# A chain of eight transformer layers on one core: a new order of the attention stages' work over two projection banks, masks and reciprocals moved between engines

## The reference, cut to what matters

```python
x = x + attn(ln(x), ln(x), 16 heads of 16, causal)      # SELF0
x = x + attn(ln(x), ctx,   16 heads of 16)              # CROSS0
x = x + mlp(ln(x))                                      # MLP0, 256 -> 1024 -> 256
x = x + attn(ln(x), ctx,   weights quantized)           # CROSS1
x = x + attn(ln(x), ln(x), logits + mask_SxS_fc0)       # SELF2
x = x + attn(ln(x), ctx,   16 heads of 16)              # CROSS2
x = x + mlp(ln(x))                                      # MLP2
x = x + attn3(ln(x), ln(ctx), 16 heads of 64, causal)   # SELF3
```

## Time and profile before

| | us |
|---|---|
| median of 3 runs (4729.28 to 4740.4) | 4730.53 |
| the profiled execution's own time | 4764.75 |
| its span in the trace | 4762.5 |
| granted TensorE clock, mean share | 0.928 |

### The profile page before, as it was taken

One profiled execution on the slowest core, in us unless ns is written; L12 is line 12 of the kernel. 1 busy time (PEld: TensorE's weight loads), 2 busy tenths in 40 slices (PEclk: granted clock), 3 DMA queues, 4 the chain that ended last, 5 costly groups with the idle time before them and its releaser, 6 DMA issues. The chain is left out here.

```text
span 4762.5 us, 66873 instructions
## 1 busy us (share of the span) xinstructions
PE 4395.3 (92%) x22610; PEld 2204.7 (46%) x22610; DVE 2705.0 (57%) x6114; ACT 2286.0 (48%) x4789; POOL 1240.6 (26%) x1277
## 2 busy tenths in 40 slices
PE   5999999999896899999999999999799899999998
PEld 3555543333463333334444443333266455555555
DVE  3555567776113677777777677777311344444443
ACT  2444456666220565654444445666421455455553
POOL 1111111111221111111111111111121566566664
PEclk8888889998797899999999999999699999999999
DMA  4433433443001443433232224443100000000000
GB/s 103 69 55 62 66 73 70 75 70 53 16 0 26 90 71 73 67 57 72 40 51 40 51 40 87 68 79 63 45 0 22 6 5 10 10 10 10 10 6 10
DMA packets 115318, 217.95 MB, mean 46 GB/s; under 512 B 22320, under 2 KB 25008, under 8 KB 113328
## 3 DMA queue, kind: packets, MB, share of 16 engines
q1 hardware_dynamic: 114992, 213.79, 24.7%
HBM read 39.11 MB, written 4.19 MB: 9 GB/s over the span
## 5 line engine op out<-in xcount | busy, mean ns | idle before, releaser
L901 ACT ACTIVATE Pr<-ST 128x512 f32<-128x512 f32 (+3 forms) x2560 | 1358.8, 564 | 1329.9 <-PE ST L486 1047.8
L486 PE MATMUL ST<-stk 50*128 50x512 f32 (+3 forms) x2560 | 1118.1, 486 | 17.1 <-ACT Pr L901 11.2
L1083 DVE TENSOR_REDUCE mx<-MX 128x1 f32<-128x512 f32 (+3 forms) x1408 | 855.9, 630 | 477.5 <-PE MX L486 469.9
L486 PE MATMUL MX<-stk 48*128 48x512 f32 (+3 forms) x1760 | 773.6, 475 | 114.3 <-DMA stk<-lo 75.2
L486 PE MATMUL OV<-Pr,V 128*32 128x512 f32 (+3 forms) x5120 | 710.5, 630 | 1.5 <-ACT Pr L901 1.5
L486 PEld LDWEIGHTS MX<-stk 48*128 48x128 f32 x1760 | 331.4, 201 | 724.7 <-issue 351.6
L1402 POOL TENSOR_SCALAR Pr<-Pr,mx 128x128 f32<-128x128 f32 (+3 forms) x512 | 548.3, 1083 | 386.7 <-DVE mx L1221 386.7
L486 PEld LDWEIGHTS ST<-stk 50*128 50x128 f32 x2560 | 462.9, 200 | 145.4 <-ACT Pr L901 112.9
L1083 DVE TENSOR_REDUCE mx<-OV 128x1 f32<-128x512 f32 (+3 forms) x640 | 400.4, 626 | 148.4 <-PE OV L486 148.2
L1336 POOL CAST mhl<-mx 128x16 fp32r<-128x16 f32 x160 | 31.9, 199 | 1475.7 <-DVE mx L1083 1124.4
L1333 POOL TENSOR_TENSOR X<-X,brow 128x1024 f32<-128x1024 f32 (+1 forms) x56 | 132.3, 2362 | 1015.9 <-DVE X L1035 1015.9
(11 more groups left out here) (134 smaller groups left out, 6781.6 us busy)
## 6 DMA issues: line engine op xcount, KB each, us to landing
stk<-hi SPq DMA_DIRECT2D x640, 128.0 KB, 3.9
stk<-lo SPq DMA_DIRECT2D x320, 128.0 KB, 4.0
misc<-misc SPq DMA_DIRECT2D x160, 128.0 KB, 3.8
sums<-misc SPq DMA_DIRECT2D x160, 128.0 KB, 4.1
misc<-in_ctx_t SPq DMA_DIRECT2D x24, 512.0 KB, 5.1
W_even<-in_w SPq DMA_DIRECT2D x4, 1024.0 KB, 6.0
W_even<-in_w SPq DMA_DIRECT2D x2, 2048.0 KB, 8.9
XH<-in_ctx_rows SPq DMA_DIRECT2D x8, 512.0 KB, 4.1
```

The costliest lines, as they stand in the source:

```text
L486: return nc.tensor.matmul(o, l, r, start=start, stop=stop)
L901: nc.scalar.activation(Pr[:, i % 2, h, q0:S], ST[h % 2][:, q0:S], ACT.Exp).then_inc(ex_done, 1)
L1083: nc.vector.tensor_reduce(m, bank[:, 0:k_n], AX.X, ALU.max).then_inc(mx_red, 1)
```

## The change

Five parts, quoted below: (a) the jobs go over two banks, LA for T0, K and V0, LB for T1, Q and V1, four jobs each, beside the turned maxima and the output projection in LB, with new places for all; LayerNorm's statistics and its GpSimd work go into the odd slot ahead of the turn; (b) DMAs in SyncE's queue are reordered, the maxima's rows last; (c) the sums are moved compactly (`few`, 128 x 32 per unit), inverted by one instruction, written to DRAM, and read back spread over 16 partitions per head; (d) in SELF0 no mask matmuls: VectorE adds `later0` in the reduction, and GpSimd clears the triangle of `Pr` after the exponential, ahead of the value product, which now is issued at j = 3 in SELF0; (e) in SELF2 VectorE masks heads 0 and 2. SELF3's mask tile is made from `later0` in one instruction; start-up loses four DMAs and two casts.

```diff
-        MASKED_BY_PE = (1, 2, 3)
+        MASKED_BY_PE = (1, 3)
...
-        J_T, J_K, J_Q, J_V, JOBS = 0, (2, 6), (3, 7), 4, 8
+        J_T, J_KQ, J_V, JOBS = 0, (1, 2), 3, 4
...
@@ SyncE, slot
                     if on["stack1"]:
-                        stack(U + 1, 1 - half, 1, GB + half)
+                        for kind in range(2):
+                            stack(U + 1, 1 - half, 1, GB + half, kind)
                     if on["tail"]:
                         move(U - 1, 1 - half, 1, GB - 1 + half)
+                        spread_rows(U - 1, 1 - half)
                     if on["b"]:
                         max_rows(U, half, 1)
-                    if on["m"]:
-                        max_rows(U + 1, 1 - half, 0)
-                    if on["a"]:
-                        stack(U + 2, half, 0, GB + 1)
-                    if on["b"]:
-                        move(U, half, 0, GB)
+                    if on["tail"]:
+                        widen(U - 1, 1 - half)
+                    if cross and half == 0 and 0 <= b < NB - 2:
+                        sp.wait_ge(lb_full, JOBS * (GB + 1))
+                        load_ctx(b + 2, c // 2)
+                    if on["a"]:
+                        for kind in range(2):
+                            stack(U + 2, half, 0, GB + 1, kind)
+                    if on["b"]:
+                        move(U, half, 0, GB)
+                    if on["m"]:
+                        max_rows(U + 1, 1 - half, 0)
...
-                    sp.dma_start(sums[64 * g:64 * g + 64, half, :], ovs[1:P:2, g, :]).then_inc(ov_moved[g], 16)
+                    sp.dma_start(few[64 * g:64 * g + 64, half, :], ovs[1:P:32, g, :].rearrange("h (c n) -> h c n", n=32)).then_inc(ov_moved[g], 16)
+
+                def spread_rows(U, half):
+
+                    sp.wait_ge(recip_done, U + 1)
+                    sp.dma_start(spread[half].rearrange("h (c n) -> (h c) n", n=32), few[:, half, :]).then_inc(spread_out, 16)
+
+                def widen(U, half):
+                    waits(sp, (spread_out, 16 * (U + 1)), (at_ready, BASE + U))
+                    rows = spread[half].rearrange("h (a n) -> h a n", a=1).broadcast_to([2 * G, HD, S])
+                    sp.dma_start(sums[:, half, :], rows).then_inc(spread_in, 16)
...
@@ TensorE, slot
-                            if at == (4, 2) and on["m"]:
+                            if at == (5, 2) and on["m"]:
+                                freed(2 + half)
                                 turn_max(U + 1, 1 - half, 0, 2 * (GB - 1 + half))
...
+                                if half == 0 and at == (0, 2):
+                                    wait(pe, la_free, JOBS * GB1 + J_T)
+                                    transpose_x(sa, ba, 0, LA).then_inc(la_full, 1)
...
+                                k_at = 1 if half == 0 else 0
+                                if at in ((k_at, 2), (k_at + 1, 2)):
...
+                                    project(LA, la_full, wq(sa, 1), half, source, i - k_at)
+                                if at in (((3, 2), (3, 3)) if half == 0 else ((2, 2), (3, 2))):
...
+                                    project(LB, lb_full, wq(sa, 0), half, hT, c)
+                                if half == 1 and i >= 4 and j == 2:
...
+                                    project_values(bank, full, wq(sa, 2), source, (i - 4) // 2, i % 2)
...
-                    pe.wait_ge(ex_done, 4 * (8 * U + i + 1))
+                    pe.wait_ge(*((cleared, 8 * U + i + 1) if causal else (ex_done, 4 * (8 * U + i + 1))))
...
@@ VectorE, slot
+                            if at == (1, 3) and on["tail"]:
+                                invert(U, 1 - half)
+                            if at in (((3, 1), (4, 2)) if half == 0 else ((2, 2), (4, 1))) and on["a"]:
+                                low_part(sa, U, half, int(i == 4))
...
+                            if at in ((6, 0), (7, 3)) and half == 1 and on["a"]:
+                                values_out(sa, GB + 1, 1 - par, i - 6)
...
+                    elif causal:
+                        k_n = P * (qt + 1)
+                        nc.vector.tensor_tensor_reduce(bank[:, 0:k_n], bank[:, 0:k_n], later0[:, S - k_n:S], 1.0, -3.0e38,
+                                                       ALU.add, ALU.max, m).then_inc(mx_red, 1)
...
+                def invert(U, half):
+
+                    for g in range(2):
+                        dve.wait_ge(ov_moved[g], 32 * U)
+                    nc.vector.reciprocal(few[:, half, :], few[:, half, :]).then_inc(recip_done, 1)
...
@@ GpSimd, slot
+                    if on["tail"] and ATTN[s - 1 if u == 0 else s][1]:
+                        clear(U - 1, 7)
...
+                def clear(U, i):
+
+                    waits(pool, (ex_done, 4 * (8 * U + i + 1)), apart=True)
+                    q0 = P * (i % 4)
+                    tile = Pr[:, i % 2, :, q0:q0 + P]
+                    nc.gpsimd.affine_select(tile, tile, [[0, G], [1, P]], ALU.is_ge, 0.0, 0, -1).then_inc(cleared, 1)
```

More of the change, by code:

```diff
@@ L558, in job @@
-                def job(GBj, k):
-                    wait(pe, la_free, JOBS * GBj + k)
-                def project(GBj, k, w, half, source, c):
-                    if c == 0:
-                        job(GBj, k)
-                    last = mm(LA[:, :], w[:, c, P * half:P * half + P], source[:, c, :], c == 0, c == NC - 1)
+                                    if i == k_at:
+                                        pe.wait_ge(la_free, JOBS * GB1 + J_KQ[half])
+                                    if half == 0 and not cross_a:
+                                        pe.wait_ge(*((la_free, JOBS * GB1 + J_T + 1) if i == k_at else (lb_free, JOBS * GB1 + J_T + 1)))
@@ L567, in project, with project_values @@
+                def project(bank, full, w, half, source, c):
+                    last = mm(bank[:, :], w[:, c, P * half:P * half + P], source[:, c, :], c == 0, c == NC - 1)
                     if c == NC - 1:
-                        last.then_inc(la_full, 1)
-                def project_values(GBj, w, source, j, t):
-                    if t == 0:
-                        job(GBj, J_V + j)
+                        last.then_inc(full, 1)
+                def project_values(bank, full, w, source, j, t):
@@ L603, in score_tile @@
                         last = mm(ST[h % 2][:, :], identr[:, :], mask_lo[:, kt, :], False, True)
-                    if causal:
-                        last = add_later(ST[h % 2][:, q0:q0 + P], lo_p, C_MK)
                     last.then_inc(st_full, 1)
-                def add_later(o, lo_p, at):
-                    rows = slice(lo_p, lo_p + 64)
-                    for part in range(2):
-                        last = mm(o, shph[rows, part, C_ID:C_ID + P], shph[rows, part, at:at + P], False, part == 1)
-                    return last
                 def values(causal, U, half, vpar, i):
@@ L1065, in slot @@
[L1065 to L1071 removed]
+                            if i == 0 and norm is not None:
+                                sn, bn = norm
+                                if j == 0 and sn > 0:
+                                    wait(dve, x_done, NB * (sn - 1) + bn + 1)
+                                statistics(NB * sn + bn, xt(bn, j), j)
@@ L1346, in slot @@
                     U, GB = UNITS * n + u, NB * n + b
+                    norm = norm_of(s, u)
+                    if norm is not None:
+                        N, rows = NB * norm[0] + norm[1], xt(norm[1], 0, NT)
+                    clears = causal and on["b"]
+                    if on["tail"] and ATTN[s - 1 if u == 0 else s][1]:
+                        clear(U - 1, 7)
                     if on["b"]:
                         maxima(U, half, 1)
-                    if half == 0 and on["a"]:
-                        sa, ba = a_of(s, u, b)
-                        layer_norm(NB * sa + ba, xt(ba, 0, NT), la_full, JOBS * GB + 2)
+                    if clears:
+                        clear(U, 0)
@@ L1352, in slot @@
+                    if norm is not None:
+                        rows_scale(N)
+                    if clears:
+                        clear(U, 1)
+                    if norm is not None:
+                        rows_centre(N, rows, lb_full, JOBS * (GB + u % 2) + J_T + 1)
+                    if clears:
+                        clear(U, 2)
+                    if norm is not None:
+                        rows_times(N)
+                    if clears:
+                        clear(U, 3)
                     if on["m"]:
@@ new lines, in slot, with biased @@
+                    if half == 1 and sums_of(s, u):
+                        biased(u - 1, b, GB)
+                    if clears:
+                        clear(U, 6)
+                    if u == UNITS:
+                        biased(u, b, GB)
+                def biased(u, b, GB):
+                    pool.wait_ge(op_evac, BASE + 2 * GB)
+                    add_bias(*end_of(s, u, b))
+                def clear(U, i):
```

(1 more changed line is left out.)

197 lines of the change are left out of this document (101 added, 96 removed).

## The result

| us | before | after |
|---|---|---|
| median of 15 runs each, taken together | 4748.07 (4729.28 to 4773.96) | 4712.69 (4694.66 to 4731.27) |
| ratio, 95% interval | | 0.9918 [0.9901, 0.9935] |
| the profiled execution: own time, span | 4764.75, 4762.5 | 4725.3, 4723.6 |
| granted TensorE clock, mean share | 0.928 | 0.923 |

The change makes the kernel 0.8% faster: 35 us came where 261 were forecast. The sign was right; the time lies above the upper end of the range.

A forecast was written before the change was run, and what follows sets the result against it. TensorE, VectorE and ScalarE were taken as nearly level, so whichever has extra work in a step decides it. Cross stages 154, SELF2 54 and SELF0 53 sum to 261 us, giving about 4470 after scaling; range 4335 to 4635.

The forecast's parts named there:

- the order of the queue: SyncE's queue: the new order of stacks, with Q's lo ready earlier, ends TensorE's slot-start wait; 1.3 us per SELF0 slot.
- Rival C: A wait replaces another: 2 us in each SELF0 slot, clock loss doubled there, time 4614; chance 0.20.
- VectorE's wait at step 1: VectorE waits at (1, 3) for compact sums: nothing or little in wide stages, 2 us per slot lost in SELF0.
- the place of the value product in SELF0: The product, issued after the next step's four products, mostly covers the clear; 0.2 left each time, 1.5 us per slot.
- The cross stages: Evened jobs and two banks for K and Q save 3.2 us per slot, 154 for three stages; bounds 2.0 and 4.4.
- SELF2: Two masked heads move to VectorE: slot falls to 43.8 us, 3.4 saved, 54 for the stage; 34 if the clock oscillates.
- a loop through the masked tile: In SELF2, heads 0 and 2 share a bank, 2.5 us per masked tile, 5.0 per step, 40 per slot, deciding its length.
- The clears: GpSimd's clear of the triangle in SELF0 was in no row; 1.3 us taken, bounds 0.6 and 5.
- rivals D and E: Slow GpSimd clears in SELF0: 5 us gives time 4675, chance 0.04; 6.5 us gives 4865, chance 0.08.
- The way by DRAM: Reciprocals written to DRAM and read back spread: from 0 (hidden) to 12.3 us after the product's evacuation.
- A: The case as forecast: time 4400 to 4540; chance 0.50.
- rival B: All waits stay hidden and SELF0's clock stays up: SELF0 gives 7 us per slot, time 4350; chance 0.15.

The follow-up runs named there:

- e1: The changed kernel with the maxima's rows of the next unit (group 0) issued ahead of `move` in SyncE's queue; 4590.63 us, ratio 0.9673 to before.
- e3: e1 with VectorE's reciprocal asked for at the end of step 2, not 1, and group 1's maxima rows ahead of the reciprocals' write; 4468.95 us.
- e8: e1 with only the reciprocal asked for one step later; the maxima's rows of group 1 stay behind the write; 4488.67 us.
- e5: e3 without GpSimd's clears in SELF0, that part of the computation left out; 4470.27 us.
- e12: e3 with SELF0's value product back at j = 1 and the product's evacuations moved with it, masks still off TensorE; 4409.81 us.
- e9: e3 with four more 128 x 128 reciprocals per slot on VectorE in the cross stages, at the old places; 4548.52 us.
- e2: e1 with TensorE masking heads 1, 2 and 3 in SELF2 again, VectorE head 0 alone; 4610.69 us.

## Why the prediction was wrong, and where it was right

**Failed: the order of the queue.** The step "Their order, with Q's lo ready at step 4 instead of 6, ends the wait at the slot's start" looked at the stacks and not at what the maxima's rows were put behind. The question "What is queued behind" was asked of the write to DRAM and not of `move`. The wait of `move` was already in SyncE's queue before; what is new is that the rows stand behind it. The new order ended the wait for lo (75.2 us in 34 places before, 8.0 in one after) and put one of 3.9 us, in every second slot and in all stages, in its place (139.4 us in 36). Rival C had this form, "a wait takes the place of another", but at 2 us in SELF0's slots only, "amid wide work" elsewhere; what it costs is 116 us (e1).

**Failed: VectorE's wait at step 1.** "In wide stages VectorE arrives near 7, sums at 8.5: nothing or little". VectorE arrived at 7.0, but the sums landed at 9.9: their DMA was issued 5.4 us into the slot instead of 4.5, behind six stack DMAs at 0.6 each that follow the late `move`, and took 4.6 instead of 4.0. A wait of 1.5 us had been taken as covered by TensorE's three banks; it came to 2.9, and TensorE stood for 1.68 of them. In CROSS0 the cost fell on the odd slots, 30.7 to 28.7; in the even ones VectorE waited 1.4 and the slot did not change. The whole is 123 us (e3 less e1), of which VectorE's place is 103 (e8), in SELF0 and the cross stages. For SELF0 the 2 per slot forecast was about right: 567.1 to 539.1 is 1.8. The cross stages, priced at nothing, lost 22, 31 and 25 us.

**Failed: the place of the value product in SELF0.** "The value product now stands after the next step's four products, about when the clear ends; 0.2 is left each time". The clear was not the cost (e5). The place was: TensorE gives up the work that kept it busy while ScalarE freed the score banks. That is 72 us (e12 less e3), 4.5 per slot, where the step had 1.5 for the clear and nothing for this. In ratios of whole runs, times 4750, the three are 116 + 123 + 65 = 304 us. That is more than the 226 missed: the forecast had charged 56 us of such losses to SELF0 (2 and 1.5 per slot), and other terms came out larger than it had them.

**The cross stages were right in size, once the waits are gone.** In e3 they take 67, 66 and 73 us less than before, 4.3 per slot: forecast 3.2, and near the upper bound 4.4 that was given for a clock that stays up, which it did (0.98). At full clock the slots of CROSS0 went from 34.2 and 31.7 to 31.1 and 28.7, 3.05 in the mean; the other 1.2 is the clock. The reciprocals' part is at most 1.7 of the 4.3 (e9). One term is missing from the sum: before, TensorE waited at slot starts for `stk<-lo` in these stages too, 12.5, 16.9 and 12.2 us, about 0.9 per slot, and in e3 not at all. So the agreement of 3.05 with the forecast's 3.2 is in part luck.

**SELF2 was right as a stage and not in its shares.** 709.0 is 44.3 per slot, forecast 43.8. Of the 45 us gained, 31 are part (e)'s as e2 prices it (1.9 per slot, and not 3.4), the rest belongs to the new order, which the forecast had at nothing here. The picture behind the 3.4, a loop through the masked tile that leaves TensorE about 1 us idle in most steps, did not come out: TensorE is busy 685.6 of 709 us, and its waits for the score banks in SELF2 of e3 are 48 in 128 steps, 0.42 us in the mean:

```profile
PE ST L510 <- ACT Pr L937: 20.2, 48, 0.6
```

Some of the loop shows beside these waits, in score products that start after the maxima's product and not with it; what bounds the stage in the main stays open.

```profile
2109.56 0.39 PE L510 MATMUL OV<-stk 48*128 48x512 f32 x1
2110.20 0.50 PE L510 MATMUL ST<-stk 50*128 50x512 f32 x1 [0.25 <-ACT Pr L937]
```

With pauses of this size and number the clock stayed at 1.00, and 45 us came where 34 had been estimated by the rule of the Trainium skill's "TensorE: Matmul & The Clock Gate" (A second HAM failure mode). The pauses of 1 us for which it was drawn on did not arise, so e3 does not test it at that size. In SELF0 the trace agrees with it: waits of 0.41 and 1.04 us among narrow tiles, and a mean clock of 0.78 in that slot.

**The clears were cheap.** Group of after, GpSimd's clear and VectorE's reciprocal:

```profile
L1445 POOL TENSOR_SCALAR_AFFINE_SELECT Pr<-Pr 128x512 f32<-128x512 f32 x128 | 81.2, 635 | 404.0 <-ACT Pr L937 404.0
...
L1144 DVE RECIPROCAL few<-few 128x32 f32<-128x32 f32 x80 | 27.9, 349 | 159.2 <-DMA few<-misc 159.2
```

635 ns is near the forecast's lower bound of 0.6, not at the 1.3 taken; rivals D and E, with 5 and 6.5 us, are out. The figure of the Trainium skill's "GPSIMD Engine Reference" (3.1) is for data-dependent branching; the 5.1 us estimated from it is eight times what this operation took here. The reciprocals fell from 299.7 to 27.9 us, forecast about 24. Behind each reduction with a mask VectorE also reads its accumulator, 141 ns, which the forecast's "697 against 678" leaves out; it fell into slack (VectorE is busy 309.6 of 466.6 us in e12's SELF0):

```profile
L1129 DVE DVE_READ_ACCUMULATOR2_ANT mx<- 128x1 f32 x512 | 72.3, 141 | 0.0
```

**The way by DRAM was hidden,** at 0 of its 0 to 12.3: in e3's CROSS0 all of TensorE's waits together are these, and none is the output projection's:

```profile
PE ST L510 <- ACT Pr L937: 10.6, 31, 0.5
PE OV L510 <- ACT misc L927: 1.0, 1, 1.0
```

**The sum.** A gain of 260 was forecast; e3, the change with its two waits taken away, gains 282 (4751.3 to 4469.0). Part of that is chance: e3 still has the third loss in it, and against their terms the cross stages gave 52 more, SELF2 9 less and SELF0 14 less. e12's 4410 lies at A's lower end, 60 above rival B's 4350, whose 7 per slot for SELF0 it reaches ((577.6 - 466.6)/16 = 6.9).

## What to carry to other kernels

When a step is moved in an in-order queue, write down for every step behind it the latest wait ahead of it, and when that wait ends, not only how long the moved step takes. Here one DMA behind a wait cost 116 us, and one wait a step too early in VectorE's queue 123, where the change with all three places put right gains 345 (e12, 4754.44 to 4409.81). Work taken from the fullest engine pays only if what stands between its other instructions still covers the engine it alternates with: in SELF0 the removed matmuls were worth 34 us, and the shift of one product by two tiles cost 72. And a result that falls short of the removed work should be read from the list of waits that are new, before any theory on contention.

## What the runs showed of the hardware

TensorE's pauses cost more than their length. Behind the wait of 3.87 us in the kernel after, the 4 us from 912 and from 916 had clocks of 0.73 and 0.84; behind that of 1.68 in e1, those from 877 and 881 had 0.74 and 0.83; e3's SELF0 slot fell to 0.50 behind 0.41 and 1.04; yet e3's SELF2, with 48 pauses of 0.42 us in the mean, stayed at 1.00. A write of 16 KB to DRAM landed in 1.4 us by the median, while the 128 KB moves between on-chip buffers of the earlier trace rows take 4.1. VectorE's reduction with the added mask costs 695 to 713 ns for 512 columns and 141 more for reading the accumulator, a plain one 684, and a reciprocal over 32 columns 349 against 940 over 128: a quarter of the width takes more than a third of the time.
